# A cross-attention and LoRA kernel on one core: the second batch's codes written in place by ScalarE alone, and half of the turned high part copied by VectorE

## The chip, the cores and the metric

The kernel runs on one core of a Trainium2 chip. The metric is the device time of one execution in microseconds (us), the median of several runs. All times below come from those runs or from one profiled execution.

## What is computed

Two batches of 1024 rows of x (2048 wide) are normalised, quantised to 8 bits and multiplied by a quantised context of 2048 x 2048 for each batch. The product is added to x. The sum is normalised again and goes through four LoRA experts of rank 16, of which a softmax over the two largest router logits weighs two. Cut to what matters:

```python
def fake_quant(x, s, z):
    q = clip(round(x / s + z), 0, 255)
    return (q - z) * s
x = x + tanh(g_xattn) * (fake_quant(layernorm(x)) @ fake_quant(ctx))
flat = layernorm(x)
logits = flat @ Wr.T
gates  = softmax(top 2 of logits, others -inf)
mid    = einsum('tf,erf->ter', flat, A)
delta  = sum_e gates[e] * einsum('ter,eor->teo', mid, B)[e] * 4
x = x + tanh(g_ffn) * delta
```

## The kernel before

**Tiles.** The 2048 rows of x are 16 tiles of 128 rows; tiles 0 to 7 belong to batch 0, tiles 8 to 15 to batch 1. `xr` is a ring of 5 buffers (`RING`): tile b lives in buffer b % 5, is loaded there, gets the product added (`add_main`, L1197), then the LoRA part (`add_delta`, L1269), and is stored from there. So tile b + 5 can be loaded only when tile b is stored: `load_x` (L247) waits for `out_stored`, and the store for `out_ready`, which `add_delta` counts. All DMAs are issued by SyncE from one list (L272 to L355), in its order.

**The product.** For each tile 16 slices of the context (k) by 4 column blocks (n) of 512 are accumulated in PSUM (`product`, L668). The operands are whole numbers in f16: the codes of x less their centre, transposed (`q1T`), and those of the context (`q2`). Tiles 0 to 3 are worked on together, slice by slice, while the context of batch 0 arrives (`rows`, L676); from tile 4 on, tile by tile (`main`, L689).

**The context rows.** A context of one batch is 32 half slices of 128 x 1024 f32, here called rows 0 to 63 (`place`, L163). A row is loaded to a staging unit (`stage`, L241: 16 units within batch 1's own part of `q2`, and one in `q1T`), ScalarE rounds it to bytes in the low halves of the 16-bit words of `c_code`, whose high halves hold 1024's pattern (`scale_row`, L443), and VectorE subtracts 1024 and the centre and writes f16 to `q2` (`code_row`, L1136). A unit is loaded again once its row is scaled. Rows 32 to 63 are needed from tile 8 on.

**x to `q1T`.** VectorE takes the statistics of x (`stats_x` for each half, L1141; `var_x`), GpSimd the power -1/2 (`power_x`, L374), VectorE the scale (`scale_of_x`, L1153); ScalarE writes the bytes (`scale_x`, L449), TensorE transposes them (`turn_q1`, L645), and ScalarE, for tiles 0 and 1 VectorE, copies them out of PSUM (`copy_q1T`, L455).

**The low-rank stage of a tile.** After `add_main`: `stats_h`, `var_h`, GpSimd's `power_h`, `bias_h` on VectorE. ScalarE writes the high part in f16 (`high_part`, L464) and the f32 value in halves (`normal_half`, L473), GpSimd the low part (`low_part`, L383). TensorE transposes both parts by halves (`turn_hi`, `turn_lo`), ScalarE copies both halves of the high part and half 0 of the low one to `hT` (`copy_hiT`, `copy_loT`, L479 to L487), VectorE half 1 of the low one (L1220). TensorE multiplies by A (`mid_hi`, `mid_lo`), VectorE ranks the gates (`rank_gates`, L1228), ScalarE takes the exponential (`gate_exp`, L489), VectorE weighs (`weigh`, L1246), TensorE transposes the gated middle (`turn_gate`, L738), VectorE splits it (`split_gate`), TensorE multiplies by B (`delta`, L748) and VectorE adds (`add_delta`). `delta(b, n)` waits until the adds up to `(b, n - 2)` are done, since it has two PSUM banks.

**The order** on every engine is written out by hand up to tile 8 and is a loop from tile 9 (`STEADY`) on. An engine works through its list strictly in order, so what stands behind a waiting step waits too.

## Time and profile before

| | us |
|---|---|
| median of 3 runs | 375.06 |
| lowest and highest | 374.97, 376.85 |
| the profiled execution | 376.49 |
| its span, first to last instruction | 374.7 |
| TensorE busy (share of the span) | 337.6 (90%) |
| VectorE busy | 290.2 (77%) |
| ScalarE busy | 251.0 (67%) |
| GpSimd busy | 96.8 (26%) |

The engines are called PE (TensorE; PEld its weight loads), DVE (VectorE), ACT (ScalarE), POOL (GpSimd) and SP (SyncE) in the rows. A row of a timeline gives the start, the duration, the engine, the line, the operation, what it writes and reads, how many alike follow one another, and in brackets the idle time before it and what ended that. Successive matmuls overlap, so their durations are longer than the distance from one start to the next. PEclk is the granted TensorE clock as a share of the full one. Idle time of an engine costs something only if the work that sets the end waits for it.

### The profile page before, as it was taken

To read this page: it belongs to the slowest core of one execution; us is meant where nothing else is said; L and a number is where in the kernel's file an instruction comes from. 1 tells how busy PE (TensorE), PEld (TensorE's weight loads), DVE (VectorE), ACT (ScalarE), POOL (GpSimd) and SP (SyncE) were. 2 spreads that over 40 slices of the span, in tenths; PEclk is the share of its full clock that TensorE was granted. 3 is DMA by queue.
4 is the path that set the end of the run, shared out by engine and by line. 5 is a ranking of instruction groups with operands and counts; after the bars stand their busy time and mean duration, and the time that the engine had idled before them with its cause. 6 is when DMAs were issued, how large, how long until landed. Compare 5 with 4: busy or idle time off the path is not lost. (4 is left out here: it accounts for less than half of the span.)

```text
span 374.7 us, 6441 instructions
## 1 busy us (share of the span) xinstructions
PE 337.6 (90%) x2372; PEld 188.7 (50%) x2372; DVE 290.2 (77%) x715; ACT 251.0 (67%) x207; POOL 96.8 (26%) x107
## 2 busy tenths in 40 slices
PE   0579989999985789999989999999999999999984
PEld 0234434445653665455555556464656565555552
DVE  4785889589996799999947796968686877866685
ACT  1769848949999699689898147464747473756150
POOL 3100430005545322033043222140505050505000
PEclk9999999999998599999999999999999999999999
DMA  7999999960046769672570524141405020202023
GB/s 218 415 420 419 420 420 420 417 278 2 3 148 239 268 247 359 213 260 87 172 258 1 193 107 152 56 170 57 170 34 192 2 115 1 114 0 114 0 86 140
DMA packets 19185, 69.17 MB, mean 185 GB/s; under 512 B 2256, under 2 KB 2256, under 8 KB 19024
## 3 DMA queue, kind: packets, MB, share of 16 engines
q1 hardware_dynamic: 19152, 68.73, 48.4%
q8 instruction: 21, 0.34, 0.4%
q14 instruction: 12, 0.10, 0.1%
HBM read 51.94 MB, written 16.78 MB: 183 GB/s over the span
## 5 line engine op out<-in xcount | busy, mean ns | idle before, releaser
L671 PE MATMUL ps_main<-q,q1T 128*128 128x512 f16 x832 | 197.4, 379 | 2.2 <-ACT q1T L460 1.6
L671 PEld LDWEIGHTS ps_main<-q,q1T 128*128 128x128 f16 x832 | 77.4, 98 | 87.2 <-issue 9.0
L446 ACT ACTIVATE c_code<-q,small_tile 128x1024 uint8<-128x1024 f32 x62 | 74.7, 1239 | 25.0 <-DVE q L1139 13.7
L470 ACT ACTIVATE h_parts<-xr,small_tile 128x2048 f16<-128x2048 f32 x15 | 31.4, 2094 | 39.4 <-DVE small_tile L1217 39.4
L390 POOL TENSOR_TENSOR h_parts<-work,h_parts 128x512 f16<-128x512 f32 x30 | 34.8, 1180 | 66.3 <-ACT work L476 66.3
L1139 DVE TENSOR_SCALAR q<-c_code,small_tile 128x1024 f16<-128x1024 f16 x64 | 37.0, 580 | 14.0 <-ACT c_code L446 13.6
L1200 DVE SCALAR_TENSOR_TENSOR xr<-ps_main,small_tile,xr 128x512 f32<-128x512 f32 x52 | 38.6, 743 | 8.1 <-PE ps_main L671 8.0
L1144 DVE BATCH_NORM_STATS2 small_tile<-xr 128x6 f32<-128x512 f32 x64 | 40.9, 680 | 5.2 <-DMA xr<-in_x 5.2
L1205 DVE BATCH_NORM_STATS2 small_tile<-xr 128x6 f32<-128x512 f32 x64 | 43.6, 687 | 0.9
L1273 DVE TENSOR_TENSOR xr<-ps_delta,xr 128x512 f32<-128x512 f32 x62 | 41.2, 680 | 3.9 <-PE ps_delta L756 3.2
L381 POOL TENSOR_TENSOR small_tile<-small_tile 128x1 f32<-128x1 f32 x16 | 9.3, 583 | 128.3 <-DVE small_tile L1213 128.3
L482 ACT COPY hT<-ps_turn 128x1024 f16<-128x1024 f16 x32 | 31.4, 1006 | 12.5 <-PE ps_turn L708 12.4
L452 ACT ACTIVATE x_byte<-xr,small_tile 128x2048 uint8<-128x2048 f32 x16 | 33.5, 2092 | 7.8 <-DVE small_tile L1159 7.8
L390 POOL TENSOR_TENSOR h_parts<-q1T,h_parts 128x512 f16<-128x512 f32 x30 | 34.1, 1160 | 1.3 <-ACT q1T L476 1.3
L754 PE MATMUL ps_delta<-lora_bT,gT_hi 128*128 128x512 f32 x60 | 30.1, 502 | 0.4 <-DVE gT_hi L1265 0.3
L460 ACT ACTIVATE q1T<-ps_gate,small_tile 128x2048 f16<-128x2048 uint8 x12 | 23.6, 1964 | 8.0 <-PE ps_gate L654 8.0
L756 PE MATMUL ps_delta<-lora_bT,gT_lo 128*128 128x512 f32 x60 | 24.4, 406 | 0.0
L642 PE MATMUL ps_main<-ident_h 128*128 128x512 f16 x47 | 12.9, 421 | 12.2 <-issue 12.2
L376 POOL TENSOR_TENSOR small_tile<-small_tile 128x1 f32<-128x1 f32 x16 | 9.5, 595 | 53.7 <-DVE small_tile L1151 53.7
L1223 DVE COPY hT<-ps_turn 128x1024 f16<-128x1024 f16 x16 | 11.0, 687 | 15.4 <-PE ps_turn L715 15.4
L671 PE MATMUL ps_turn<-q,q1T 128*128 128x512 f16 x64 | 18.1, 380 | 4.8 <-DVE q L1139 3.1
L727 PE MATMUL ps_mid<-a_parts,hT 128*128 128x136 f16 x256 | 20.8, 229 | 0.9 <-ACT hT L482 0.9
(122 smaller groups left out, 415.1 us busy)
## 6 DMA issues: line engine op xcount, KB each, us to landing
q<-in_ctx SPq DMA_DIRECT2D x62, 512.0 KB, 10.9
xr<-in_x SPq DMA_DIRECT2D x32, 512.0 KB, 4.9
out_x<-xr SPq DMA_DIRECT2D x30, 512.0 KB, 3.4
h_parts<-in_B SPq DMA_DIRECT2D x1, 1024.0 KB, 16.5
q1T<-in_ctx SPq DMA_DIRECT2D x2, 512.0 KB, 6.4
out_x<-xr SPq DMA_DIRECT2D x4, 256.0 KB, 2.3
xr<-in_A SPq DMA_DIRECT2D x1, 544.0 KB, 16.2
small_tile<-in_params SPq DMA_DIRECT2D x1, 3.0 KB, 2.6
```

Source lines behind the costliest of these rows:

```text
L390: nc.gpsimd.tensor_tensor(h_lo[:, half(h)][:, part], work[h][:, part], h_hi[:, half(h)][:, part], ALU.subtract).then_inc(h_lo_ready, 1)
L446: nc.scalar.activation(c_byte[:, i % 2, :], stage(i), ACT.Identity, bias=par[:, 3:4], scale=inv_s[:, 1:2]).then_inc(row_scaled, 1)
L452: nc.scalar.activation(x_byte[:, :], xr[:, b % RING, :], ACT.Identity, bias=q_scale[:, 1:2], scale=q_scale[:, 0:1]).then_inc(x_scaled, 1)
L470: nc.scalar.activation(h_hi[:, :], xr[:, b % RING, :], ACT.Identity, bias=h_bias[:, b % 2:b % 2 + 1], scale=h_rstd[:, b % 2:b % 2 + 1]).th ...
L482: nc.scalar.copy(hT[:, h, :, :], as16(ps_turn[h], F16).rearrange("p (k m) -> p k m", m=P)).then_inc(hiT_ready, 1)
L671: mm = pe.matmul(product_bank(b, n)[:, :], q1T_of(b)[:, k, :], q2[:, batch(b), k, cols(n)], start=(k == 0), stop=(k == KT - 1))
L754: pe.matmul(ps_delta[n % 2][:, :], gT_hi[:, :], lora_bT[:, cols(n)], start=True, stop=False)
L1139: nc.vector.tensor_scalar(q2[:, batch_of, k, half(h)], c_code[:, i % 2, :], low_centre[:, :], None, ALU.add).then_inc(row_coded, 1)
L1144: nc.vector.bn_stats(x_stats[:, n, :], xr[:, b % RING, cols(n)]).then_inc(x_stats_done, 1)
L1200: nc.vector.scalar_tensor_tensor(out=x1, in0=product_bank(b, n)[:, :], scalar=gain[:, 0:1], in1=x1, op0=ALU.mult, op1=ALU.add).then_inc(x1 ...
L1205: nc.vector.bn_stats(h_stats[:, b % 2, n, :], xr[:, b % RING, cols(n)]).then_inc(h_stats_done, 1)
L1273: nc.vector.tensor_tensor(x1, src[:, :], x1, ALU.add).then_inc(out_ready, 1)
```

## The change

Three things change, and with them the lists of all engines.

1. **Codes of batch 1.** Rows 32 to 63 are no longer coded by VectorE. GpSimd fills each of batch 1's 16 slices of `q2` with a pattern that is 1024 in both f16 halves (`clear`), and ScalarE writes the bytes straight into the low halves, so `q2` holds 1024 + code. The product of batch 1 is then too large by (1024 + centre) times the sum of the tile's x codes less their centre, one number for each row of x. ScalarE sums the codes (`sum_codes`, two activations a tile with an accumulator), VectorE makes the shift (`shift_of_row`), and `add_delta` subtracts it for tiles 8 to 15. Since the number is constant along a row, it drops out of the second normalisation.
2. **Staging.** Eight units in `q2`, one in `c_code` and one in `q1T` serve rows 32 to 63 (18 units in all with batch 0's). The slices of batch 1 lie in the order `slot_of`; slices 8 to 15 are cleared first, the others when their units are empty (`left_by`).
3. **The turned high part.** Half 1 of it is copied by VectorE (`copy_hiT` on VectorE), half 0 by ScalarE as before.

```diff
-            def copy_hiT(b, h):
-                act.wait_ge(hi_turned, 2 * b + h + 1)
-                wait(act, lo_used, 2 * (b - 1) + h + 1)
-                nc.scalar.copy(hT[:, h, :, :], as16(ps_turn[h], F16).rearrange("p (k m) -> p k m", m=P)).then_inc(hiT_ready, 1)
+            def copy_hiT(b):
+                act.wait_ge(hi_turned, 2 * b + 1)
+                wait(act, lo_used, 2 * b - 1)
+                nc.scalar.copy(hT[:, 0, :, :], as16(ps_turn[0], F16).rearrange("p (k m) -> p k m", m=P)).then_inc(hiT_ready[0], 1)
...
+            def copy_hiT(b):
+                dve.wait_ge(hi_turned, 2 * b + 2)
+                wait(dve, lo_used, 2 * b)
+                nc.vector.tensor_copy(hT[:, 1, :, :], as16(ps_turn[1], F16).rearrange("p (k m) -> p k m", m=P)).then_inc(hiT_ready[1], 1)
...
+            def clear(k):
+                pool.wait_ge(row_scaled, left_by[k])
+                nc.gpsimd.memset(q2_pair[:, slot_of[k], :], TWO_BASES).then_inc(place_cleared, 1)
...
             def scale_row(i):
                 act.wait_ge(row_loaded[unit_of[i]], 16 * (unit_turn(i)[1] + 1))
-                wait(act, row_coded, i - 1)
-                nc.scalar.activation(c_byte[:, i % 2, :], stage(i), ACT.Identity,
+                batch_of, k, h = place(i)
+                if batch_of == 0:
+                    wait(act, row_coded, i - 1)
+                    byte = c_byte[:, i % 2, :]
+                else:
+                    act.wait_ge(place_cleared, k + 1)
+                    byte = q2_byte[:, slot_of[k], half(h), 0]
+                nc.scalar.activation(byte, stage(i), ACT.Identity,
                                      bias=par[:, 3:4], scale=inv_s[:, 1:2]).then_inc(row_scaled, 1)
...
+            def sum_codes(b):
+                act.wait_ge(x_scaled, b + 1)
+                wait(act, row_summed, b - PER_B)
+                for h in range(2):
+                    wait(act, codes_summed, 2 * (b - PER_B) + h)
+                    nc.scalar.activation(byte_copy[:, :], x_byte[:, half(h)], ACT.Identity, bias=0.0, scale=1.0,
+                                         accum_out=code_sums[:, h:h + 1]).then_inc(codes_summed, 1)
...
+            def shift_of_row(b):
+                dve.wait_ge(codes_summed, 2 * (b - PER_B) + 2)
+                nc.vector.scalar_tensor_tensor(out=row_sum[:, :], in0=code_sums[:, 0:1], scalar=code_sums[:, 1:2], in1=x_zeros[:, :],
+                                               op0=ALU.add, op1=ALU.add).then_inc(row_summed, 1)
+                dve.wait_ge(row_summed, b - PER_B + 1)
+                nc.vector.tensor_scalar(shift[:, b % RING:b % RING + 1], row_sum[:, :], code_gain[:, :], None, ALU.mult).then_inc(shift_ready, 1)
...
-                nc.vector.tensor_tensor(x1, src[:, :], x1, ALU.add).then_inc(out_ready, 1)
+                if b < PER_B:
+                    nc.vector.tensor_tensor(x1, src[:, :], x1, ALU.add).then_inc(out_ready, 1)
+                else:
+                    dve.wait_ge(shift_ready, b - PER_B + 1)
+                    nc.vector.scalar_tensor_tensor(out=x1, in0=src[:, :], scalar=shift[:, b % RING:b % RING + 1], in1=x1,
+                                                   op0=ALU.subtract, op1=ALU.add).then_inc(out_ready, 1)
```

The unit numbers of rows 32 to 63, by which loads wait:

```diff
-        late_unit = (8, 9, 10, 11, 12, 13, 14, 15, 16, 13, 14, 15, 14, 15, 15, 16)
-        unit_of = [i % KT for i in range(3 * KT)] + list(late_unit)
+        late_unit = (0, 1, 2, 3, 4, 5, 6, 7, 16, 17, 0, 1, 2, 3, 4, 5, 16, 17, 0, 1, 2, 3, 16, 17, 0, 1, 16, 17, 16, 17, 16, 17)
+        unit_of = [i % KT for i in range(2 * KT)] + list(late_unit)
```

The list of SyncE around the first stores was `load_row(47)`, `store(0, 0)`, `load_row(48)`, `store(0, 1)`, `load_x(5)`, `load_row(49)`, and is now `load_row(52)`, `store(0, 0)`, `store(0, 1)`, `load_row(53)`, `load_x(5)`.

How the lists moved is shown at three places. The first is VectorE where it first meets x of tile 5 (`BN_STATS ... x2` is one `stats_x`, the rows on `ps_delta` are `add_delta`, `hT` is a copy out of PSUM). Before:

```order
L1139 TENSOR_SCALAR q2<-c_code,small_tile 128x1024
L1273 TENSOR_TENSOR xr<-ps_delta0,xr 128x512
L1273 TENSOR_TENSOR xr<-ps_delta1,xr 128x512
L1217 TENSOR_SCALAR small_tile<-small_tile 128x1
L1144 BN_STATS small_tile<-xr 128x6 x2
L1273 TENSOR_TENSOR xr<-ps_delta0,xr 128x512
L1223 COPY hT<-ps_turn1 128x1024
L1273 TENSOR_TENSOR xr<-ps_delta1,xr 128x512
L1144 BN_STATS small_tile<-xr 128x6 x2
```

and after the change:

```order
L1323 CAST gT_hi<-ps_gate 128x128
L1325 TENSOR_TENSOR gT_lo<-ps_gate,gT_hi 128x128
L1197 BN_STATS small_tile<-xr 128x6 x2
L1332 TENSOR_TENSOR xr<-ps_delta0,xr 128x512
L1276 COPY hT<-ps_turn1 128x1024
L1332 TENSOR_TENSOR xr<-ps_delta1,xr 128x512
L1270 TENSOR_SCALAR small_tile<-small_tile 128x1
L1332 TENSOR_TENSOR xr<-ps_delta0,xr 128x512
```

The code of a row is gone, and the statistics of x5 moved from behind the two adds of tile 1 to ahead of them and of the copy.

The second is TensorE ahead of the first product of tile 5 (`ps_main0<-q2,q1T`; `x_byte` is `turn_q1(5)`, `gated` is `turn_gate(3, 6)`). Before:

```order
L754 MATMUL ps_delta1<-lora_bT,gT_hi 128x512
L756 MATMUL ps_delta1<-lora_bT,gT_lo 128x512
L654 MATMUL ps_gate<-ident_h,x_byte 128x128 x8
L708 MATMUL ps_turn0<-ident_h,h_parts 128x128 x8
L708 MATMUL ps_turn1<-ident_h,h_parts 128x128 x8
L671 MATMUL ps_main0<-q2,q1T 128x512 x5
L746 MATMUL ps_gate<-ident_f,gated 128x128
L671 MATMUL ps_main0<-q2,q1T 128x512
L727 MATMUL ps_mid<-a_parts,hT 128x136 x8
```

and after the change:

```order
L753 MATMUL ps_turn0<-ident_h,h_parts 128x128 x8
L780 MATMUL ps_mid<-a_parts,hT 128x68 x8
L753 MATMUL ps_turn1<-ident_h,h_parts 128x128 x8
L699 MATMUL ps_gate<-ident_h,x_byte 128x128 x8
L772 MATMUL ps_mid<-a_parts,hT 128x136 x8
L791 MATMUL ps_gate<-ident_f,gated 128x128
L772 MATMUL ps_mid<-a_parts,hT 128x136 x8
L760 MATMUL ps_turn0<-ident_h,h_parts 128x128 x8
L716 MATMUL ps_main0<-q2,q1T 128x512 x4
L799 MATMUL ps_delta0<-lora_bT,gT_hi 128x512
```

The middle products of tile 4, the gate of tile 3 and a transpose of tile 4's low part moved ahead of tile 5's first product.

The third is ScalarE from the low part of tile 3 (`hT<-ps_turn0`) to `copy_q1T(5)` (`q1T<-ps_gate`); `x_byte` is `scale_x(5)`, `mids` is `gate_exp(3)`, `h_parts` is `high_part(4)`. Before:

```order
L487 COPY hT<-ps_turn0 128x1024
L452 ACTIVATE x_byte<-xr,small_tile 128x2048
L470 ACTIVATE h_parts<-xr,small_tile 128x2048
L491 ACTIVATE small_tile<-mids,small_tile 128x4
L460 ACTIVATE q1T<-ps_gate,small_tile 128x2048
```

and after the change:

```order
L541 COPY hT<-ps_turn0 128x1024
L524 ACTIVATE h_parts<-xr,small_tile 128x2048
L497 ACTIVATE x_byte<-xr,small_tile 128x2048
L536 COPY hT<-ps_turn0 128x1024
L530 ACTIVATE work0<-xr,small_tile 128x1024
L545 ACTIVATE small_tile<-mids,small_tile 128x4
L514 ACTIVATE q1T<-ps_gate,small_tile 128x2048
```

The high part of tile 4 moved ahead of `scale_x(5)`, and a copy and a half of tile 4 moved ahead of `copy_q1T(5)`; `gate_exp(3)` stands ahead of it in both.

## Rows read from the trace of the kernel before

**Rows 1.** Page, part 1: busy time and share of the span, each engine

```profile
PE 337.6 (90%) x2372; PEld 188.7 (50%) x2372; DVE 290.2 (77%) x715; ACT 251.0 (67%) x207; POOL 96.8 (26%) x107
```

**Rows 2.** Timeline of PE: start us, duration us, what, [idle before]

```profile
108.53 2.10 PE L671 MATMUL ps_main<-q,q1T 128*128 128x512 f16 x9
...
121.78 0.64 PE L735 MATMUL ps_mid<-a_parts,hT 128*128 128x68 f16 x8 [3.81 <-DVE hT L1223]
...
126.61 0.48 PE L746 MATMUL ps_gate<-ident_f,gated 128*128 128x128 f32 x1 [2.49 <-DVE gated L1257]
...
136.29 1.24 PE L671 MATMUL ps_main<-q,q1T 128*128 128x512 f16 x5 [1.26 <-ACT q1T L460]
```

**Rows 3.** Windows: stretch, length, busy per engine, PEclk, DMA share, GB/s

```profile
115.00:125.00 10.00, 4.79 (x52) 3.61 (x48) 6.71 (x19) 7.31 (x8) 4.68 (x5) 0.70 0.93 342
```

**Rows 4.** Timeline of DVE around the statistics of x5

```profile
107.72 0.67 DVE L1273 TENSOR_TENSOR xr<-ps_delta,xr 128x512 f32<-128x512 f32 x1
...
119.25 1.28 DVE L1144 BATCH_NORM_STATS2 small_tile<-xr 128x6 f32<-128x512 f32 x2 [3.16 <-DMA xr<-in_x]
...
121.64 0.68 DVE L1273 TENSOR_TENSOR xr<-ps_delta,xr 128x512 f32<-128x512 f32 x1
...
123.43 0.29 DVE L1230 TENSOR_REDUCE ps_mid<-ps_mid 128x68 f32<-128x136 f32 x1
...
124.79 0.26 DVE L1149 BATCH_NORM_AGGREGATE small_tile<-small_tile 128x2 f32<-128x24 f32 x1
```

**Rows 5.** Timeline of ACT, steady part

```profile
338.28 2.10 ACT L470 ACTIVATE h_parts<-xr,small_tile 128x2048 f16<-128x2048 f32 x1 [5.24 <-DVE small_tile L1217]
```

**Rows 6.** Groups by line and form: busy us, mean ns, idle before

```profile
L446 ACT ACTIVATE c_code<-q,small_tile 128x1024 uint8<-128x1024 f32 x62 | 74.7, 1239 | 25.0 <-DVE q L1139 13.7 <-DMA q<-in_ctx 11.3
...
L1273 DVE TENSOR_TENSOR xr<-ps_delta,xr 128x512 f32<-128x512 f32 x62 | 41.2, 680 | 3.9 <-PE ps_delta L756 3.2 <-PE ps_delta L767 0.6
...
L1200 DVE SCALAR_TENSOR_TENSOR xr<-ps_main,small_tile,xr 128x512 f32<-128x512 f32 x52 | 38.6, 743 | 8.1 <-PE ps_main L671 8.0
L1139 DVE TENSOR_SCALAR q<-c_code,small_tile 128x1024 f16<-128x1024 f16 x64 | 37.0, 580 | 14.0 <-ACT c_code L446 13.6
...
L482 ACT COPY hT<-ps_turn 128x1024 f16<-128x1024 f16 x32 | 31.4, 1006 | 12.5 <-PE ps_turn L708 12.4
...
L1223 DVE COPY hT<-ps_turn 128x1024 f16<-128x1024 f16 x16 | 11.0, 687 | 15.4 <-PE ps_turn L715 15.4
...
L360 POOL MEMSET c_code<- 128x2048 f16 x1 | 1.8, 1804 | 0.3 <-POOLq L1597 0.3
```

**Rows 7.** DMA, us to landing, issued at 108.42, 132.47, 106.51, 114.05, 126.83

```profile
out_x<-xr SPq DMA_DIRECT2D x1, 512.0 KB, 5.6
...
out_x<-xr SPq DMA_DIRECT2D x1, 512.0 KB, 3.7
...
out_x<-xr SPq DMA_DIRECT2D x1, 512.0 KB, 2.6
...
xr<-in_x SPq DMA_DIRECT2D x1, 512.0 KB, 5.2
...
xr<-in_x SPq DMA_DIRECT2D x2, 512.0 KB, 4.6
```

**Rows 8.** Timeline of PE, steady part: middle product of two tiles

```profile
327.11 0.64 PE L727 MATMUL ps_mid<-a_parts,hT 128*128 128x136 f16 x8
...
346.86 0.64 PE L727 MATMUL ps_mid<-a_parts,hT 128*128 128x136 f16 x8
347.34 0.61 PE L715 MATMUL ps_turn<-ident_h,h_parts 128*128 128x128 f16 x8
```

**Rows 9.** Timeline of DVE: a slow `code_row`

```profile
47.56 2.48 DVE L1139 TENSOR_SCALAR q<-c_code,small_tile 128x1024 f16<-128x1024 f16 x1
```

**Rows 10.** Waits of PE: waited for, us in total, times, longest

```profile
PE ps_main L671 <- ACT q1T L460: 1.6, 2, 1.3
...
PE ps_mid L727 <- ACT hT L482: 0.9, 1, 0.9
```

715 lines of the change are left out of this document (359 added, 356 removed).

## Prediction

> **What bounds the kernel now.** The page first: TensorE is busy for 90% of the span and VectorE for 77% [rows 1], so a change that takes work off VectorE pays only where TensorE waits for it. The timeline of TensorE shows where that is. From tile 9 on it runs almost without a gap, 19.8 us a tile (the first middle product of one tile starts at 327.11, that of the next at 346.86 [rows 8]), and nothing that this change does there can move the end. The one large hole lies between the last product of tile 4, issued until 110.5 us [rows 2], and the first of tile 5 at 136.29 [rows 2]; in it TensorE works only on the low-rank stage of tiles 1 to 4, with waits of 3.81, 2.49 and 1.26 us. The window over its worst part adds that the granted clock was 0.70 there in the mean [rows 3]; 1.00 is the level of 2.4 GHz and 0.50 that of 1.2 GHz, and the fall came after the engine had stood idle behind its wait of 3.81 us. The hole costs some 10 us of idleness and some 4 of half speed.
>
> What ends the hole is tile 5's x. It goes into the ring buffer of tile 0, so it is a round trip: the last `add_delta` of tile 0 (107.72 us, ends 108.39), the store, the load, the statistics at 119.25 after a wait of 3.16 us for the DMA [rows 4], then the scale, ScalarE's `scale_x(5)`, the transposes and ScalarE's `copy_q1T(5)`. Tiles 6 and 7 take the same trip. I count from T, the time at which VectorE finds the first half of x5: T = 119.25 before, and tile 5 starts at T + 17.0.
>
> **What hides and what does not.** Removed: 32 `code_row` of 0.58 us = 18.6 us of VectorE, and 16 ScalarE copies of 1.01 = 16.1 us. Added: 16 VectorE copies of 0.69 = 11.0 us [rows 6], and 16 `sum_codes` activations of 1024 elements, for which the nearest row is the coding activation of as many elements, 1.24 us [rows 6]: 20 us of ScalarE, most of it in the steady part, where that engine stands idle 5.24 us before each tile's high part [rows 5]. I cost both at nothing; the cover is TensorE's 19.8 us a tile, and if it were gone each pair would cost 2.5 us. The 16 clears on GpSimd have one near row, a memset of 2048 elements in 1.80 us [rows 6]; a clear has half the elements and as many bytes, so 0.9 to 1.8 us, and I take 0.95. Ten fall before the hole ends, in time GpSimd has idle, ahead of low parts which then wait for ScalarE anyway: nothing.
>
> Up to 85 us the new order gains little. The early x scales come before waiting rows, which brings tile 1 forward by 1.5 us, but tiles 2 and 3 start 2 us later, and VectorE's work on B is as long as before. I make the start of tile 4 0.6 us earlier (between 1.5 earlier and 1.5 later). It is lost again at once, because of the next term.
>
> **The step that decides.** ScalarE now scales rows 42 to 44 before `copy_loT(1)`; eight more products stand ahead of tile 0's last delta. Counting TensorE from 86.0 us (0.6 before the 86.6 of now) with 0.22 us a product (nine in 2.10 [rows 2]), I get the last `add_delta` of tile 0 at 108.5, as before. The store then takes between 3.7 us and 5.6 (a context row was issued just ahead of that one; now row 53 comes just behind the store), the load 4.6 to 5.2 [rows 7]. So T lies at 116.9 to 119.5; I take 117.5, nearer the short end since nothing is ahead of the store.
>
> But VectorE's order around T is another one. Before, `stats_x(5, 0)` stood behind `add_delta(1, 0)` and `(1, 1)`; now it stands ahead of both and of `copy_loT(2)`. They are ready 3 us before T and are queued behind a DMA. After T come: statistics 1.2, add 0.6, copy 0.6, add 0.6, bias 0.15, add 0.6, `rank_gates(2)` 1.36 (from 123.43 to 124.79 [rows 4]), add 0.65: `add_delta(1, 3)` ends at T + 5.8. Before it ended at 122.32, which is T + 3.1 [rows 4]. So x6, whose load waits for tile 1's store, comes at T + 5.8 + 3.7 + 4.6 and some issue time = T + 14.7. `stats_x(6, 0)` again stands ahead of the last `add_delta` of its round, of `rank_gates(3)`, `copy_hiT(4)` and `weigh(3)`. ScalarE has `gate_exp(3)` ahead of `copy_q1T(5)`, and TensorE has `turn_gate(3, 6)`, `mid_hi(4, 1)` and `turn_lo(4, 0)` ahead of tile 5. That makes: x6 T + 14.7, statistics 1.2, but VectorE, with TensorE at half speed, arrives a little later: add ends T + 17.4, rank 18.8, copy 19.4, weigh 20.3, then gate transpose 0.17, middle product 0.48 (346.86 to 347.34 [rows 8]) and transposes 0.45, in all 1.1. Tile 5 starts at T + 21.4 = 138.9, 2.6 us later than before. Work that stood behind this point is now ahead of it: two middle products 0.96, a gate 0.17, one set of transposes 0.45 = 1.6 us. **Term 1: 2.6 - 1.6 = +1.0 us.**
>
> The third trip: `add_delta(2, 3)` ends at T + 17.4, x7 lands at T + 25.9, `stats_x(7, 0)` stands ahead of `add_delta(3, 0)`, which ends at T + 27.8. TensorE reaches `delta(3, 2)`, which waits for it, at T + 25.0 and holds the rest of tile 5's first block behind it. Before, the third load was issued early enough. **Term 2: +2.8 us.**
>
> After this TensorE finds everything ready: x8 and x9 have room, and low parts and copies of hi come earlier, so TensorE's wait of 0.9 us for ScalarE's copy of hi goes, and the shorter of the two for q1T (1.6 in sum, the longer 1.3: 0.3) [rows 10]. **Term 3: -1.2 us.** In the tail the copy on VectorE replaces the second ScalarE copy, which was hidden by an add; and the last adds take the form with a scalar, 0.74 in place of 0.68 us [rows 6] (three of tile 14 and the four last). **Term 4: +0.4 us.**
>
> Sum +3.0. The profiled execution took 376.49 us (span 374.7), 1.4 above the median of 375.06, so it would become 379.5 and the median **378.0 us**.
>
> **A rule weighed.** One `code_row` took 2.48 us at 47.56 [rows 9], the mean is 0.58 [rows 6], and in the slow one GpSimd was working. So the clears between 66 and 76 us could lengthen the last `code_row`s of batch 0. TensorE needs row 31 at 77.4 us and it is coded at 74.6, so 2.8 us are covered; five clears of 0.95 that each hold a code back cost 4.8 - 2.8 = 2.0 us. The Trainium skill ("SBUF — State Buffer", section "SBUF: two separate sides") calls the pair of ports that VectorE and GpSimd share an exclusive lock: whichever starts first keeps the pair for its whole instruction and the other blocks. By this rule the clears would block VectorE, and the sum would be +5.0, not +3.0, if all five collided; by the rows each one meets a short instruction now and then, so I leave it at nothing.
>
> **Rivals.**
> - *The round trips are short (faster).* A store took 2.6 us when nothing ran beside it [rows 7]. With stores of 2.6 and loads of 3.8 each trip is 1.9 us shorter than I took. T = 115.6, tile 5 at T + 19.3 = 134.9, so term 1 is -3.0, term 2 +0.9, with terms 3 and 4 a sum of -2.9: 372.2 us. If VectorE never waited for x at all (trip under 5.1 us, the work between `add_delta(0, 3)` and `stats_x(5, 0)`), tile 5 starts at 131 and it is 367 us. For it: VectorE does lose 18.6 us of work in the stretch where it was fullest. Against: x5 took 10.9 us from add to statistics. It turns at trips of 7.3 us. Chance 0.22.
> - *No change that can be measured.* Trips about 1 us shorter than taken, or the start gains its 1.5 us, 375 us. Chance 0.20.
> - *My forecast,* 0.40, own range 376.9 to 380.
> - *The clock stays low.* Before, it fell after a wait of 3.81 us [rows 2, 3] and was full again when tile 5 began. In the new order TensorE idles 4 us (T + 16 to 20) just before tile 5, so its first products may run at 1.2 GHz and take twice the time. Work of 3 us at half speed adds 3: 381 us. Chance 0.12.
> - *The port lock,* 380 us. Chance 0.06.
>
> **How the numbers follow.** A measurement of this kernel can tell 0.5%, 1.9 us, from no change. Slower: 0.40 + 0.12 + 0.06 = 0.58. Same 0.20, faster 0.22. The range reaches down to the short trips and up to the low clock with 1 us more for the landing of x5; it leaves out a VectorE that never waits, and above 382 a low clock together with a collision at the port.
>
> **What would show it.** VectorE's `stats_x(5, 0)`, `(6, 0)` and `(7, 0)` waiting for DMA by 3 to 4, up to 2, and 2 to 3 us; the first product of tile 5 near 139 us and `delta(3, 2)` waiting for VectorE's add; GpSimd's memset near 0.95 us; nothing of 32 late `code_row`; tiles 9 to 15 at 19.8 us each. I am wrong if tile 5 starts before 135 us, or if x7 has landed when VectorE comes to it. If tiles 9 to 15 take longer than 19.8 us each, `sum_codes` or the shift is not hidden.

## The result and the profile after

The change makes the kernel slower: median 380.79 us of 4 runs (379.26 to 382.64) against 375.62 of 4 of the kernel before (374.97 to 376.85); ratio 1.0142, 95% interval 1.0118 to 1.0166, so +5.2 us where 2.9 were forecast (378.0 against 375.06). The profiled execution after took 379.26 us (span 377.4), the one before 376.49: +2.8 between the two profiles, forecast +3.0. The median of 380.79 lies above the own range of the forecast, 376.9 to 380. Executions more than 1.5% above the fastest of their kernel are left out of all ratios; there are three, in three kernels below, and each is named with its time. Two things need an explanation: where the time between the two profiles goes, and why the medians differ by more than the profiles do.

The page's busy times, to hold against [rows 1]:

```profile
PE 337.2 (89%) x2372; PEld 188.4 (50%) x2372; DVE 291.5 (77%) x717; ACT 254.3 (67%) x223; POOL 110.1 (29%) x123
```

VectorE is as busy as before (290.2 then) although 32 codes left it. They took only 14.5 us with them (37.0 before, 22.5 now), and the 16 copies added 10.9, the two small operations of `shift_of_row` 3.4 and the longer adds 2.0. Its timeline where it waits for a load of x or ends tile 0, to hold against [rows 4]:

```profile
106.62 1.50 DVE L1332 TENSOR_TENSOR xr<-ps_delta,xr 128x512 f32<-128x512 f32 x2 [0.16 <-PE ps_delta L801]
...
116.72 1.29 DVE L1197 BATCH_NORM_STATS2 small_tile<-xr 128x6 f32<-128x512 f32 x2 [3.31 <-DMA xr<-in_x]
...
131.91 1.29 DVE L1197 BATCH_NORM_STATS2 small_tile<-xr 128x6 f32<-128x512 f32 x2 [2.68 <-DMA xr<-in_x]
...
141.79 1.29 DVE L1197 BATCH_NORM_STATS2 small_tile<-xr 128x6 f32<-128x512 f32 x2 [2.04 <-DMA xr<-in_x]
...
155.84 1.29 DVE L1197 BATCH_NORM_STATS2 small_tile<-xr 128x6 f32<-128x512 f32 x2 [2.03 <-DMA xr<-in_x]
...
170.59 1.29 DVE L1197 BATCH_NORM_STATS2 small_tile<-xr 128x6 f32<-128x512 f32 x2 [3.95 <-DMA xr<-in_x]
```

Before, one such wait stood here (3.16 us); now there are five, for x5 to x9. TensorE's timeline, to hold against [rows 2, 8, 10]:

```profile
111.73 0.62 PE L760 MATMUL ps_turn<-ident_h,h_parts 128*128 128x128 f16 x8 [2.74 <-POOL h_parts L402]
...
118.75 0.47 PE L799 MATMUL ps_delta<-lora_bT,gT_hi 128*128 128x512 f32 x1 [1.76 <-DVE xr L1332]
...
124.63 0.33 PE L791 MATMUL ps_gate<-ident_f,gated 128*128 128x128 f32 x1 [2.62 <-DVE gated L1315]
...
136.81 1.07 PE L772 MATMUL ps_mid<-a_parts,hT 128*128 128x136 f16 x8 [5.62 <-DVE gated L1315]
...
139.64 1.28 PE L716 MATMUL ps_main<-q,q1T 128*128 128x512 f16 x4
...
143.81 0.47 PE L799 MATMUL ps_delta<-lora_bT,gT_hi 128*128 128x512 f32 x1 [0.16 <-DVE xr L1332]
...
158.52 0.47 PE L799 MATMUL ps_delta<-lora_bT,gT_hi 128*128 128x512 f32 x1 [1.32 <-DVE xr L1332]
...
329.73 0.64 PE L772 MATMUL ps_mid<-a_parts,hT 128*128 128x136 f16 x8
...
349.48 0.64 PE L772 MATMUL ps_mid<-a_parts,hT 128*128 128x136 f16 x8
```

TensorE waits 1.76 us for an add that was queued behind x5, 2.62 and 5.62 for gates queued behind x5 and x6, 1.32 for an add behind x8. Tile 5's first product is at 139.64 (before 136.29). In the steady part one tile still takes 349.48 - 329.73 = 19.75 us. Windows, the first as in [rows 3]:

```profile
115.00:125.00 10.00, 5.38 (x60) 3.77 (x60) 8.04 (x23) 8.68 (x8) 5.68 (x6) 0.94 0.65 229
...
132.00:140.00 8.00, 3.19 (x26) 2.96 (x27) 7.14 (x25) 5.09 (x6) 3.73 (x4) 0.58 0.67 233
```

The clock is higher than before from 115 to 125 (0.94 against 0.70) and is low later, 0.58 from 132 to 140, just ahead of tile 5. The groups that answer to [rows 6]:

```profile
L1332 DVE TENSOR_TENSOR xr<-ps_delta,xr 128x512 f32<-128x512 f32 x32 | 21.5, 680 | 3.1 <-PE ps_delta L801 2.9
...
L1335 DVE SCALAR_TENSOR_TENSOR xr<-ps_delta,small_tile,xr 128x512 f32<-128x512 f32 x30 | 21.6, 742 | 0.6 <-PE ps_delta L812 0.6
...
L1184 DVE TENSOR_SCALAR q<-c_code,small_tile 128x1024 f16<-128x1024 f16 x32 | 22.5, 707 | 7.4 <-ACT c_code L490 7.2
...
L506 ACT ACTIVATE byte_copy<-x_byte 128x1024 uint8<-128x1024 uint8 x16 | 16.8, 1050 | 0.3
...
L1281 DVE COPY hT<-ps_turn 128x1024 f16<-128x1024 f16 x16 | 10.9, 682 | 0.8 <-PE ps_turn L753 0.7
...
L408 POOL MEMSET q<- 128x1024 f32 x16 | 15.3, 969 | 26.3 <-ACT c_code L490 16.3 <-ACT q L490 10.0
```

A ledger of TensorE made from each trace says where the time went. It has the idle times in the brackets of its timeline, summed by stretch, and for the half clock the sum over 1 us windows of busy time x (1 - PEclk). The first stretch ends with the wait ahead of tile 4's first product (at 86.61 before, near 85.5 in the others). Stretches with a difference, us:

| profile (span) | idle 0-87 | idle 87-111 | idle 111-144 | half clock 111-144 | idle 144-165 | idle 165-200 |
|---|---|---|---|---|---|---|
| before (374.7) | 18.7 | 0.2 | 9.3 | 4.2 | 0.0 | 1.2 |
| changed (377.4) | 17.4 | 0.0 | 13.7 | 3.4 | 1.3 | 0.4 |
| changed, repeated (378.5) | 17.7 | 0.0 | 12.9 | 4.8 | 1.3 | 1.7 |
| four places undone (372.3, its fastest execution) | 17.0 | 0.0 | 9.2 | 4.4 | 0.8 | 0.2 |

Over the whole span the two kinds of loss add up to 36.5, 38.8, 40.9 and 34.1 us: differences to before of +2.3, +4.4 and -2.4, where the spans differ by +2.7, +3.8 and -2.4. The ledger accounts for the spans within 0.6 us. The changed kernel gains 1.3 us up to the start of tile 4, and loses more than that in the hole and just behind it.

### The profile page after: what moved, and what is told of

Same layout as the page of the kernel before. It is cut to its first block, busy times and chain, and to the rows that moved or that the text cites. A ratio compares the mean times of both kernels' runs of the same rounds, so it can differ in the third digit from the quotient of the medians.

```text
span 377.4 us, 6514 instructions
## 1 busy us (share of the span) xinstructions
PE 337.2 (89%) x2372; PEld 188.4 (50%) x2372; DVE 291.5 (77%) x717; ACT 254.3 (67%) x223; POOL 110.1 (29%) x123
## 4 chain that ended last, share of the span: by engine, by line
PE 61%; DMA 16%; DVE 14%; SPq 5%; issue 2%; ACT 1%; DVEq 0%; ACTq 0%
PE ps_main L716 38%; DMA xr<-in_x 6%; DMA out_x<-xr 5%; DMA xr<-in_A 4%; SPq L280 4%; PE ps_mid L772 3%; PE ps_turn L760 3%; PE ps_turn L753 3%; PE ps_delta L799 3%; PE ps_delta L801 3%; DVE small_tile L1197 3%; PE ps_turn L716 2%; DVE xr L1332 2%; DVE xr L1253 2%; PE ps_delta L716 2%
## 5 line engine op out<-in xcount | busy, mean ns | idle before, releaser
L402 POOL TENSOR_TENSOR h_parts<-work,h_parts 128x512 f16<-128x512 f32 x30 | 34.1, 1160 | 65.2 <-ACT work L530 65.2
L1197 DVE BATCH_NORM_STATS2 small_tile<-xr 128x6 f32<-128x512 f32 x64 | 40.9, 680 | 15.3 <-DMA xr<-in_x 15.3
L490 ACT ACTIVATE c_code<-q,small_tile 128x1024 uint8<-128x1024 f32 x32 | 38.4, 1237 | 17.1 <-DMA q<-in_ctx 9.0
L393 POOL TENSOR_TENSOR small_tile<-small_tile 128x1 f32<-128x1 f32 x16 | 8.8, 550 | 108.9 <-DVE small_tile L1266 108.9
L402 POOL TENSOR_TENSOR h_parts<-q1T,h_parts 128x512 f16<-128x512 f32 x30 | 34.1, 1160 | 1.5 <-ACT q1T L530 1.5
L1184 DVE TENSOR_SCALAR q<-c_code,small_tile 128x1024 f16<-128x1024 f16 x32 | 22.5, 707 | 7.4 <-ACT c_code L490 7.2
L536 ACT COPY hT<-ps_turn 128x1024 f16<-128x1024 f16 x16 | 16.1, 1003 | 14.0 <-PE ps_turn L753 14.0
L687 PE MATMUL ps_main<-ident_h 128*128 128x512 f16 x47 | 12.9, 424 | 12.5 <-issue 12.5
L1332 DVE TENSOR_TENSOR xr<-ps_delta,xr 128x512 f32<-128x512 f32 x32 | 21.5, 680 | 3.1 <-PE ps_delta L801 2.9
L490 ACT ACTIVATE q<-q,small_tile 128x1024 uint8<-128x1024 f32 x20 | 23.7, 1232 | 0.0
L772 PEld LDWEIGHTS ps_mid<-a_parts,hT 128*128 128x128 f16 x256 | 18.0, 103 | 10.1 <-issue 5.8
L408 POOL MEMSET q<- 128x1024 f32 x16 | 15.3, 969 | 26.3 <-ACT c_code L490 16.3
```

The source lines that it names most:

```text
L402: nc.gpsimd.tensor_tensor(h_lo[:, half(h)][:, part], work[h][:, part], h_hi[:, half(h)][:, part], ALU.subtract).then_inc(h_lo_ready, 1)
L490: nc.scalar.activation(byte, stage(i), ACT.Identity, bias=par[:, 3:4], scale=inv_s[:, 1:2]).then_inc(row_scaled, 1)
L772: mm = pe.matmul(ps_mid[:, 0:2 * J], hT[:, h, k, :], a_parts[:, kk, :, :].rearrange("p c j -> p (c j)"), start=(kk == 0), stop=False)
L1197: nc.vector.bn_stats(x_stats[:, n, :], xr[:, b % RING, cols(n)]).then_inc(x_stats_done, 1)
L1332: nc.vector.tensor_tensor(x1, src[:, :], x1, ALU.add).then_inc(out_ready, 1)
```

## The experiments

All times are medians; the kernel before was run beside each group (375.15 to 375.63 us in the medians of five groups).

**The changed kernel again.** No edit.

> The changed kernel, unchanged, once more. Its profiled execution took 379.26 us and the three others 380.45 to 382.64, at mean granted clocks of 0.984 and 0.976 to 0.982, while the profiled execution of the kernel before was at 0.982. Two explanations of why the medians differ by 5.2 us where the two profiles differ by 2.8. (a) Clock: in the long hole before tile 5 TensorE's clock stays at its lower level for longer in some executions; then a longer execution shows a lower mean clock, 1 us longer for each 0.003 of it (0.003 x 377), and its extra time lies between 110 and 150 us. (b) The transfers of x land later in some executions; then the clock says nothing and the waits of VectorE for x5 to x8 (3.31, 2.68, 2.04, 2.03 us) are longer in the new profile. I expect (a) in part: median 380.5 (379.3 to 382), lower clocks with the longer executions.

Measured: 379.98 us (379.62 to 380.22), ratio 1.0121 (1.0103 to 1.0140). The clock does not order its executions: 380.22 us at 0.986, 380.11 at 0.977. So (a), the clock, falls. The profile equals the first one within 0.5 us up to 169 us and is then 1.1 us later through one place. VectorE and TensorE:

```profile
171.68 1.29 DVE L1197 BATCH_NORM_STATS2 small_tile<-xr 128x6 f32<-128x512 f32 x2 [4.99 <-DMA xr<-in_x]
```

```profile
143.90 0.47 PE L799 MATMUL ps_delta<-lora_bT,gT_hi 128*128 128x512 f32 x1 [0.58 <-DVE xr L1332]
...
158.58 0.47 PE L799 MATMUL ps_delta<-lora_bT,gT_hi 128*128 128x512 f32 x1 [1.29 <-DVE xr L1332]
...
176.43 0.65 PE L772 MATMUL ps_mid<-a_parts,hT 128*128 128x136 f16 x8 [1.46 <-DVE hT L1281]
```

x9 was found at 171.68 (170.59 in the first profile, above), the copy of tile 5's high part is queued behind it, and TensorE waited 1.46 us for the copy, in the first profile not at all. A fifth wait on x costs nothing or a microsecond, depending on the load. That speaks for (b).

**One place of VectorE's list undone.**

```diff
-            stats_x(5, 0)
             add_delta(1, 0)
             copy_loT(2)
             add_delta(1, 1)
+            stats_x(5, 0)
```

> Only the first of the four places is undone: VectorE's statistics of the first half of x5 stand behind both adds and the copy that are ready, as in the kernel before. Theory (head of line): the adds (1,0) to (1,2) and the copy no longer wait 3.31 us; add (1,3) ends about 2 us sooner, at about T + 3.5 in place of T + 5.7, the load of x6 is issued at 124.3 in place of 126.3, and x6 lands 2 us sooner, so that VectorE's wait at x6 shrinks from 2.68 to about 1 and tile 5 starts at 137.5 in place of 139.64: 2 us less than the repeated kernel. Rival (the landing of x5 alone counts, since TensorE's hole is ended by x5's own path): the start of tile 5 moves by less than 0.5 us, and the time by less than 0.5 us.

Measured: 379.42 (377.99 to 382.58), ratio 1.0124 (1.0091 to 1.0157): the median is 0.6 less than that of the repeated kernel, but by the ratios (1.0121 there) the two are not told apart. x5 is no longer waited for and x6 hardly, as the theory said:

```profile
130.23 1.29 DVE L1197 BATCH_NORM_STATS2 small_tile<-xr 128x6 f32<-128x512 f32 x2 [0.29 <-DMA xr<-in_x]
...
140.42 1.29 DVE L1197 BATCH_NORM_STATS2 small_tile<-xr 128x6 f32<-128x512 f32 x2 [2.34 <-DMA xr<-in_x]
...
143.47 1.29 DVE L1197 BATCH_NORM_STATS2 small_tile<-xr 128x6 f32<-128x512 f32 x2 [1.18 <-DMA xr<-in_x]
...
155.47 1.29 DVE L1197 BATCH_NORM_STATS2 small_tile<-xr 128x6 f32<-128x512 f32 x2 [1.98 <-DMA xr<-in_x]
```

But x7 and its second half are now waited for 2.34 and 1.18 us, where the repeated kernel waited 2.13: the first middle product of tile 4 came 1.7 us sooner (135.12 against 136.79) and most of that was lost again at the next x. The theory's mechanism holds, its gain of 2 us does not.

**Four places undone.**

```diff
-            stats_x(6, 0)
             add_delta(2, 3)
             rank_gates(3)
             copy_hiT(4)
             weigh(3)
+            stats_x(6, 0)
...
-            stats_x(7, 0)
             add_delta(3, 0)
-            stats_x(7, 1)
             add_delta(3, 1)
+            stats_x(7, 0)
+            stats_x(7, 1)
...
-            stats_x(8, 0)
             add_main(5, 2)
             add_delta(4, 0)
             stats_h(5, 2)
             add_delta(4, 1)
+            stats_x(8, 0)
```

and x5's as above.

> All four places: the statistics of the first halves of x5, x6, x7 and x8 stand behind the work that is ready (two adds and a copy; an add, the ranking, a copy and the weighing; two adds; an addition of the product, two adds and their statistics). No wait goes, only what is queued behind it. Theory: the three trips are each shorter by what their last add waited for, tile 5 starts at about 137, TensorE's waits of 1.32 at delta (4, 2) and 0.16 at delta (3, 2) go; 4 us less than the repeated kernel, so about 376.5, 1 us above the kernel before. Rival 1 (the order of VectorE is not what costs: DMA landings or ScalarE's and TensorE's own orders hold tile 5 back): within 1 us of the repeated kernel. Rival 2 (x is now found later, its scale comes later, and ScalarE waits): slower than the repeated kernel by 1 to 2 us.

Measured: 375.82 (374.10 to 378.26, and one of 380.59), ratio 1.0018 (0.9995 to 1.0040): 4.2 us less than the repeated kernel, where 4 were expected. Both rivals fall. Of VectorE's waits for x5 to x8 0.33 us is left, and TensorE's hole is shorter:

```profile
116.71 1.29 DVE L1197 BATCH_NORM_STATS2 small_tile<-xr 128x6 f32<-128x512 f32 x2 [0.33 <-DMA xr<-in_x]
```

```profile
121.28 1.03 PE L760 MATMUL ps_turn<-ident_h,h_parts 128*128 128x128 f16 x8 [3.02 <-POOL h_parts L402]
...
132.87 0.63 PE L772 MATMUL ps_mid<-a_parts,hT 128*128 128x136 f16 x8 [2.49 <-DVE gated L1315]
...
135.27 1.91 PE L716 MATMUL ps_main<-q,q1T 128*128 128x512 f16 x4
```

Every instruction, place in memory and load is as in the changed kernel; only what stood behind the statistics of a late x now stands ahead. So the order of VectorE's list was the whole loss, as far as the runs can tell (the interval of this ratio takes in 1).

**Part 3 undone.** A `copy_hiT1` on ScalarE takes half 1 of the high part, behind `normal_half(b, 1)` (tile 4: `(4, 0)`), and VectorE's copies go.

> Only part 3 of the change is undone: half 1 of the turned high part is copied by ScalarE again (16 x 1.0 us), everything else and every other place in the lists as in the changed kernel. Theory: both engines have room in the steady part, so tiles 9 to 15 stay at 19.8 us; in the hole VectorE saves two copies of 0.69 that stand ahead of the weighing of tiles 2 and 3 while ScalarE gets two of 1.0 beside a wait of 2.0 us: within 1 us of the repeated kernel. Rival (the copy belongs to what costs the time, since VectorE is full in the hole): 1 to 1.5 us less than the repeated kernel. Rival (it is this part that pays, ScalarE being the later one): 1 to 3 us more.

Measured: 384.88 (382.45 to 385.43), ratio 1.0252 (1.0230 to 1.0273): 4.9 more, 2.2 between the two profiles. The theory falls and the last rival holds: in the order of the changed kernel, and with ScalarE's copy placed as here, this part pays. Its size is above what that rival said (1 to 3), and over half of it lies outside the profile. TensorE waits twice for ScalarE's copy of half 1 (L541 is the new `copy_hiT1`), of tiles 5 and 6:

```profile
176.39 0.65 PE L787 MATMUL ps_mid<-a_parts,hT 128*128 128x136 f16 x8 [0.52 <-ACT hT L541]
...
192.96 0.65 PE L787 MATMUL ps_mid<-a_parts,hT 128*128 128x136 f16 x8 [2.12 <-ACT hT L541]
```

The first of them stands where the repeated kernel waited 1.46 us for VectorE's copy, so only the second is new. Besides, the first middle product of tile 4 began 1.0 us later (137.77 against 136.79).

**Five places undone**: behind x5 to x8 also x9.

```diff
-            stats_x(9, 0)
             add_main(6, 1)
-            stats_x(9, 1)
             stats_h(6, 1)
-            var_x(9)
             copy_hiT(5)
+            stats_x(9, 0)
+            stats_x(9, 1)
+            var_x(9)
```

> As the kernel with four places undone, and a fifth: both halves of the statistics of x9 stand behind the second addition of tile 6's product, its statistics and the copy of tile 5's high part. In the profile of the repeated kernel VectorE waited 4.99 us for x9 (3.95 in the changed kernel's first profile), ended at 171.68 (170.59), and TensorE waited 1.46 us for the copy behind it (not at all in the first profile): the 1.1 us between these two executions. Theory: this fifth wait is why executions of the same kernel differ, so with it harmless the median comes down to the lowest execution of the four-place kernel, 374.3 (median there 375.8, lowest 374.1), and the executions lie closer together: under 1.5 us between the lowest and the next to highest. Rival (the spread is the clock's or the transfers' elsewhere): median 375.8 again, spread as wide.

Measured: 375.90 (374.60 to 379.64), ratio 1.0024 (0.9996 to 1.0051). The rival holds: the median is unchanged and the spread no narrower, although the profile shows no wait of VectorE for x at all. Once the other four were in order, x9 did not matter.

**TensorE kept busy in the hole.**

```diff
+                pe.wait_ge(x1_ready, parts_done(4, 2))
+                keep_busy(9)
                 turn_lo(2, 0)
...
+                keep_busy(9)
                 turn_lo(3, 0)
...
+                keep_busy(8)
                 mid_hi(4, 0)
```

> As the kernel with five places undone, and TensorE is kept busy in its hole with 9, 9 and 8 products of 512 columns into a bank that is free (ahead of the transposes of the low parts of tiles 2 and 3, where it waits 2.74 and 3.02 us for GpSimd, and ahead of tile 4's first middle product, where it waits 2.49 us): 0.22 us each, 2.0 us a time at 2.4 GHz. In the four-place kernel the granted clock was at half from 121 to 127 and from 134 to 137 us, some 9 us of which TensorE worked some 7. If the half clock costs what it seems (work that takes twice as long, 3.5 us, part of it hidden in waits): 1.5 to 3 us less than the five-place kernel, and a mean clock of 0.99. Rival (the chain through ScalarE and GpSimd sets the hole, and TensorE's work in it is beside the path): within 0.5 us. Rival (a product that is issued late holds the transposes back): up to 1 us more.

Measured: 376.13 (375.65 to 378.48), ratio 1.0023 (1.0003 to 1.0044), no gain. Windows of this kernel, then of the one with five places:

```profile
126.00:140.00 14.00, 12.31 (x120) 8.13 (x119) 11.02 (x32) 13.57 (x11) 5.07 (x5) 0.98 0.68 237
```

```profile
126.00:140.00 14.00, 11.45 (x94) 8.35 (x94) 11.05 (x31) 13.26 (x11) 5.07 (x5) 0.78 0.71 254
```

The granted clock rose from 0.78 to 0.98 in the second half of the hole, the mean of the execution from 0.979 to 0.993, and the time did not follow. Tile 4's first middle product did begin 1.1 us earlier (132.99 against 134.09), but in this profile x7 came late again: VectorE waited 1.64 and 0.78 us for it and TensorE 1.65 us for a copy behind it, which the other profile does not have. That TensorE's work in the hole stands beside the path fits the medians; whether the products held x7 back or it was late by itself was not tested.

**The first clears twice.**

```diff
+                if k < 8:
+                    nc.gpsimd.memset(q2_pair[:, slot_of[k], :], TWO_BASES).then_inc(first_clear, 1)
+                    pool.wait_ge(first_clear, k + 1)
                 nc.gpsimd.memset(q2_pair[:, slot_of[k], :], TWO_BASES).then_inc(place_cleared, 1)
```

> The changed kernel with the first eight clears done twice, eight more memsets of 0.95 us on GpSimd between 62 and 76 us, where VectorE codes the last rows of batch 0. Theory (as forecast: the clears cost nothing): within 0.5 us of the repeated kernel, start of tile 4 at 85.5 to 86.0. Rival (GpSimd and VectorE shut each other out): code_row, which rose from 580 to 707 ns in the mean with eight clears beside it, rises again by some 100 ns, tile 4 starts 0.5 to 2 us later and the kernel takes as much more.

Measured: 381.12 (380.48 to 383.37), ratio 1.0148 (1.0122 to 1.0175), about 1 us more than the repeated kernel, tile 4 at 86.49 in place of 85.55. That is the rival's size, but not its cause: the codes took 656 ns in the mean, less than 707. The profile shows the microsecond in GpSimd's queue:

```profile
69.45 0.21 DVE L1213 TENSOR_SCALAR small_tile<-small_tile 128x1 f32<-128x1 f32 x1 [2.44 <-POOL small_tile L389]
...
73.39 0.55 DVE L1188 TENSOR_SCALAR q<-c_code,small_tile 128x1024 f16<-128x1024 f16 x1 [1.63 <-ACT c_code L494]
```

`power_x(4)` stands behind the clears, VectorE waited 2.44 us for it (0.43 in the repeated kernel) and ScalarE's `scale_x(4)` 1.78 us (there not at all). What clear and code do to each other stands in single rows. In the repeated kernel ScalarE's semaphore released both at once, and the code (VectorE) took 1.25 us where 0.47 is usual, the clear (GpSimd) 0.95:

```profile
73.73 1.25 DVE L1184 TENSOR_SCALAR q<-c_code,small_tile 128x1024 f16<-128x1024 f16 x1 [0.21 <-ACT c_code L490]
```

```profile
73.76 0.95 POOL L408 MEMSET q<- 128x1024 f32 x1 [0.51 <-ACT c_code L490]
```

With clears back to back the code at 73.39 began first and took 0.55; the clear that began beside it took the longer time:

```profile
73.60 1.23 POOL L410 MEMSET q<- 128x1024 f32 x1
```

**Without the sums.** The subtraction of each row's constant is left out for batch 1 (`sum_codes`, `shift_of_row`, and `add_delta` in its plain form).

> The changed kernel without ScalarE's sums of codes, without the shift and with the plain add everywhere: the subtraction of the constant of each row is left out for batch 1. Theory (both hidden in the steady part, 0.4 us in the tail): 0 to 0.6 us less than the repeated kernel, tiles 9 to 15 at 19.8 us each in both. Rival (the wait of VectorE for the sum of tile 8 or ScalarE's 2.3 us ahead of copy_loT(5) and copy_hiT(6) cost something between 165 and 195 us): 1 to 2 us less, and TensorE's waits of up to 0.3 us there gone.

Measured: 380.74 (378.91 to 382.15), ratio 1.0127 (1.0101 to 1.0153): no difference that can be told, against 1.0121. The sums are hidden, as the theory said.

**Loads of x first.** On the kernel with five places:

```diff
-            load_row(56)
             store(2, 0)
             store(2, 1)
             load_x(7, 0)
             load_x(7, 1)
+            load_row(56)
```

> As the kernel with five places undone, and on SyncE the load of row 56 stands behind the stores of tile 2 and the load of x7 in place of ahead of them (issued near 137 in place of 125.4 us; ScalarE scales it at 149.4). In the profile of the kernel with five places x7 had landed when VectorE came to it, in that with keep-busy products it had not: a wait of 1.64 us at 139.97 and of 0.78 for its second half, with the copy of tile 4's low part behind them and TensorE behind that for 1.65 us. Theory (the executions of these kernels differ by when x7 lands, and its round trip shares the queue with x6's load and row 56): the store of tile 2 lands 1 us sooner, x7 too, and the executions come together near the lowest of the five-place kernel: median 375.0 (it was 375.9, lowest 374.6), spread under 1.5 us without one outlier. Rival (the spread is elsewhere): median 375.9, executions from 374.6 to 379 as before.

Measured: 375.77 (373.41 to 376.57), ratio 0.9998 (0.9978 to 1.0018). Four executions were below 374.3, three of them lower than any until then, eight above 375.6: unclear, nearer the rival.

**ScalarE's rows behind the halves.** On the kernel with five places:

```diff
-            scale_row(45)
             normal_half(2, 0)
             copy_hiT(2)
+            scale_row(45)
...
-            scale_row(48)
             normal_half(3, 0)
             copy_hiT(3)
+            scale_row(48)
```

> As the kernel with five places undone, and ScalarE scales rows 45 and 48 behind the first half of the normalised value and the copy of the high part of tiles 2 and 3, in place of ahead of them. TensorE's two longest waits of the hole now are for GpSimd's low parts of these tiles (2.76 us at 111.68, 2.60 at 121.61), GpSimd waits for ScalarE's half, and ScalarE is busy without a gap. Theory (ScalarE's list sets the hole once VectorE's doesn't): each of the two waits is shorter by the 1.13 us of a row, everything to tile 5 comes 1 to 2 us sooner: median 374.3 (373.5 to 375). Rival (x5 and x6, not the low parts, set when tile 5 starts): within 0.5 us of 375.9.

Measured: 377.43 (375.94 to 380.53, and one of 382.22), ratio 1.0060 (1.0033 to 1.0088): 1.5 more. TensorE's waits for the low parts did shrink (1.61 and 1.87 us), but x5, its load issued at 112.29, was found 1.7 us later than with four places undone (118.44 against 116.71), and the weighing is still behind it. The edit has a side effect that I had not seen: row 53 is loaded to the staging unit of row 45, so its load waits until row 45 is scaled. It went out at 110.31 in place of 108.44, right ahead of x5's. The kernel with both edits shows the same (row 53 at 110.41, x5 found at 119.17).

```profile
118.44 1.29 DVE L1197 BATCH_NORM_STATS2 small_tile<-xr 128x6 f32<-128x512 f32 x2 [2.19 <-DMA xr<-in_x]
```

```profile
124.55 0.47 PE L791 MATMUL ps_gate<-ident_f,gated 128*128 128x128 f32 x1 [3.63 <-DVE gated L1315]
```

**Part 3 alone**, on the kernel before: `copy_hiT` of half 1 on VectorE, placed near the times of ScalarE's copies.

> The kernel before with part 3 of the change alone: half 1 of the turned high part is copied by VectorE (16 copies of 0.69 us in place of 16 of 1.0 on ScalarE), its codes and their places as before. Taking this part out of the changed kernel cost 4.9 us (384.9 against 380.0). Theory (ScalarE is the busiest engine from 86 to 126 us, 25.00 of 25 and 12.06 of 15 us, so its copies stand on the path): 1 to 4 us less than the kernel before. Rival (VectorE is as full there, 23.4 of 25 us, and its copy delays the adds by which x5 comes in): within 1 us of it. Rival (the 4.9 us belonged to the order of the changed kernel alone): 1 to 2 us more than before.

Measured: 378.24 (376.98 to 379.58), ratio 1.0083 (1.0063 to 1.0103): 2.9 more than before. TensorE waited for my first placement, behind a code and statistics, and tile 5 then began as late as before the change:

```profile
95.34 0.65 PE L717 MATMUL ps_mid<-a_parts,hT 128*128 128x136 f16 x8 [2.84 <-DVE hT L1218]
...
136.54 1.24 PE L661 MATMUL ps_main<-q,q1T 128*128 128x512 f16 x5 [1.26 <-ACT q1T L460]
```

So this part's worth hangs on its place in the list; alone and placed like this it costs, in the changed kernel it pays. The profiled execution took 376.98 us, only 0.5 more than the one before, so where most of the 2.9 lies is not shown.

**The last two edits together** (loads first, rows behind).

> The last two edits together on the kernel with five places undone: row 56 loaded behind x7, rows 45 and 48 scaled behind the halves. If both theories hold, 373.5 and the lowest of all kernels here, faster than the kernel before by 0.5%. If only ScalarE's order counts, as the kernel with that edit alone; if neither, 375.9.

Measured: 376.54 (375.64 to 378.68), ratio 1.0037 (1.0021 to 1.0053): neither theory.

**x6, x7 and x8 undone, x5 left.**

> The changed kernel with the places of x6, x7 and x8 undone and that of x5 left. With x5's place alone undone the time was 379.4 (0.6 less than the repeated kernel), with all four 375.8. Theory (each late x holds back the adds by which the next x comes, and x6's place holds the most: an add, the ranking, a copy and the weighing): most of the 4.2 us come back, median 377 (376.3 to 377.8), tile 5's first middle product near 135.5 in place of 136.8. Rival (only all four together help, since any one left moves the wait on): above 378.5. Rival (x5's place costs nothing beside the others): 375.8.

Measured: 378.36 (377.36 to 379.83), ratio 1.0083 (1.0059 to 1.0108). x5's place alone gives 0.6 (within the noise), the other three 1.6, all four 4.2. They do not add. The profile fits the reading that one late x that is left in the way holds the next ones back: VectorE waits 2.74 us for x5 and again 2.60 for x7, and TensorE then 1.78 for the copy behind x7.

**Row 53 behind x5's load**, on top of row 56's place.

> As the kernel with five places undone and row 56 behind x7's load (median 375.8; executions in two groups, four from 373.4 to 374.3 and eight from 375.6 to 376.6), and also row 53 behind the load of x5 (it is scaled near 141 us). x5's first half landed 4.6 to 6.6 us after its load was issued at 112.1 to 112.8. Theory (row 53's transfer, issued at 108.5 beside the store, and x5 share the 16 DMA engines; the two groups are an early and a late x5): x5 lands near 4.6 us after its issue in all executions, which move to the lower group: median 374.0. Rival (the groups come from elsewhere, or the store alone sets it): 375.8 in two groups.

Measured: 375.25 (373.87 to 379.22), ratio 1.0002 (0.9979 to 1.0026). The groups have run into each other; 0.5 less is within what can be told. Its profile, of an execution of 376.49, shows a loss elsewhere. ScalarE:

```profile
156.72 1.24 ACT L490 ACTIVATE q<-q1T,small_tile 128x1024 uint8<-128x1024 f32 x1 [4.29 <-DMA q1T<-in_ctx]
...
162.70 1.24 ACT L490 ACTIVATE q<-q1T,small_tile 128x1024 uint8<-128x1024 f32 x1 [1.66 <-DMA q1T<-in_ctx]
...
163.85 2.08 ACT L497 ACTIVATE x_byte<-xr,small_tile 128x2048 uint8<-128x2048 f32 x1
```

TensorE:

```profile
165.98 0.62 PE L699 MATMUL ps_gate<-ident_h,x_byte 128*128 128x128 f16 x8 [2.28 <-ACT x_byte L497]
```

ScalarE waited for two rows' loads, x8's scale stood behind the second, and TensorE waited 2.28 us for it.

**x5 behind the weighing**, on top: `stats_x(5, 0)` and `(5, 1)` behind `weigh(2)` and `copy_hiT(3)`.

> As the kernel just before, and both halves of x5's statistics stand behind the weighing of tile 2 and the copy of tile 3's high part, so that no ranking or weighing is queued behind x5. Theory: the time no longer depends on when x5 lands up to about 120 us; TensorE's wait for the gate of tile 2 (1.25, 1.75, 3.63, 4.26 us in four profiles, in the order of x5's landing) is under 1 us, x5's scale is as early as before since ScalarE is at the high part of tile 4 till 127: median 374.0, spread under 1.5 us. Rival (x5's own path is now 1 to 2 us later and tile 5 waits for it): 376 to 377.

Measured: 375.72 (373.40 to 376.45), ratio 1.0003 (0.9986 to 1.0020). The wait for the gate of tile 2 went, and TensorE waited 2.43 us for the split of that gate instead. Theory and rival are both half right; no gain.

**And ScalarE's rows behind the halves**, on top.

> As the kernel just before, and rows 45 and 48 scaled behind the halves and copies of tiles 2 and 3, the edit that made 377.4 of 375.9 before. Theory (it failed there because x5, which then stood ahead of the weighing, landed late, and TensorE waited 3.63 us for the weighing): now it brings the 1.1 us of a row at TensorE's two waits for GpSimd: median 373.0, faster than the kernel before by over 0.5%. Rival (the edit costs by itself, for example by holding back the rows' loads): 1 us or more above the kernel just before.

Measured: 376.46 (374.56 to 377.90), ratio 1.0028 (1.0009 to 1.0046). The rival: that edit costs by itself, here with row 53 loaded behind x5 and no ranking or weighing queued behind x5.

**x8's scale ahead of row 61's**, on the kernel with rows 53 and 56 moved.

```diff
-            scale_row(61)
             scale_x(8)
+            scale_row(61)
```

> As the kernel with five places undone and rows 56 and 53 behind the loads of x (375.25, profile at 376.49), and ScalarE scales x8 ahead of row 61. There the scale of x8 began at 163.85 after ScalarE had waited 1.66 us for row 61; its factors were ready at 158.9 and ScalarE was free at 161.0. TensorE's turn of x8 waited 2.28 us at 165.98. Theory (in this region a row's load, not x, is what is waited for): the scale begins at 161.0, TensorE's wait goes, high part of tile 5 is as before: 1 to 2 us less, median 373.8, faster than the kernel before by 0.4%. Rival (TensorE's next wait, for the low part of tile 5 behind the high part and row 62, takes it over): within 0.5 us of 375.25.

Measured: 374.93 (373.49 to 376.12, and one of 712.88, which no profile explains), ratio 0.9991 (0.9978 to 1.0004). TensorE's wait at x8 is gone; 0.3 less than without the edit.

**And row 59 loaded ahead of x8.**

> As the kernel just before, and on SyncE row 59 is loaded ahead of x8 in place of behind it: ScalarE waited 4.29 us for row 59 (2.75 to 4.29 in four profiles) and VectorE came to x8 without a wait. Theory: ScalarE's wait for row 59 falls to about 2 us, rows 60 and 61 follow 1 to 2 us sooner, and since the sums, row 62 and tile 5's high part stand behind them the median is 0.5 us below the kernel just before. Rival (x8 lands 1.5 us later and VectorE waits for it at 153.7): 0.5 us above it.

Measured: 374.83 (372.76 to 375.67), ratio 0.9985 (0.9968 to 1.0001), the lowest of all, and not told from the kernel before (its interval reaches 1). ScalarE's wait for row 59 fell to 0.63 us, and a wait of 3.00 for row 60 took its place.

## Why the prediction was wrong, and what in it was right

**Right: sign, place and mechanism.** By the steps of the forecast: tile 4 began at 85.53 (said 86.0); the last add of tile 0 ended at 108.1 (106.62 + 1.50; said 108.5); x5 was found at T = 116.72 after a wait of 3.31 (said 117.5, 3 to 4); x6 at T + 15.2 after 2.68 (said up to 2, landing at T + 14.7); x7 at T + 25.1 after 2.04 (said T + 25.9, 2 to 3). Tile 5 began at 139.64 (said 138.9), a tile of the steady part takes 19.75 us (said 19.8), a clear 969 ns (said 950), and the sums cost nothing. That VectorE's order is the cause is shown, not only read from the profile: four places undone give back 4.2 us of 4.5.

**The first step that failed** is the sentence "After this TensorE finds everything ready: x8 and x9 have room". I followed the round trip for three tiles and stopped. x8 came late (a wait of 2.03, and 1.32 of TensorE behind it), x9 too (3.95, and in the repeated execution 4.99 and 1.46 of TensorE). That is 1.3 us in one profile and 2.8 in the other, where the forecast has nothing.

**The second was the way from the profile to the median.** I took the new median 1.4 us below the new profile, as it was before. But the offset belongs to the execution. The profile before lay above its median, the profile after was the lowest of its four runs. Why executions of these kernels differ is shown in one pair (x9's landing, 1.1 us), and making x9 harmless did not narrow the spread, so the rest is open. The clock does not order them. The size of this error is not firm either: the same kernel run again had a median of 379.98.

**Between the profiles the sum came out (+2.8 for +3.0), and that was luck.** Its terms were off by more, and cancel.

- Term 1 (+1.0) was too small. Tile 5 began 3.35 us later (139.64 for 136.29), which less the 1.6 of work moved ahead is +1.7. Behind the weighing I had a gate, one middle product and transposes, 1.1 us. It is 2.83 us (136.81 to 139.64): the other middle product of tile 4 waits for the weighing as well, and all four ran at half clock.
- That is the mechanism of the rival that I gave 0.12, but it is not what made the kernel slower: from 111 to 144 us the half clock cost 3.4 us in the one profile and 4.8 in the other, and 4.2 before the change.
- Term 2 (+2.8) was hardly there. Tile 5 began later against T, so TensorE waited only 0.16 us for tile 3's add behind x7 (0.58 in the repeated kernel).
- Terms 1 and 2 were 3.8 together and came to 1.9. The ledger agrees: up to 144 us TensorE lost 2.0 us more than before (2.9 in the repeated kernel).
- Term 3 (-1.2): the two waits that it names are gone (0.94 and 0.30 us in the kernel before, at 191.10 and 175.03). In their place stand new ones of 0.43 in one profile and 1.71 in the other, x9's among them.
- Term 4 (+0.4) was about 0.1: from the weighing of tile 14 (VectorE at 356.09, before at 353.47) to the end of the span 21.3 us against 21.2.
- With the 1.3 us behind x8 these come to 2.5, and the spans differ by 2.7.

**The port.** I gave a rival of 380 us a chance of 0.06. Its mechanism is there: a code that is released together with a clear takes 1.25 us in place of 0.47, and one that began first takes 0.55 while the clear takes 1.23 in place of 0.95. By the rule weighed in the forecast (the Trainium skill, "SBUF — State Buffer", section "SBUF: two separate sides") whichever starts first holds the pair of ports for its whole instruction. The second pair of rows agrees; in the first the code's record starts 0.03 us before the clear's (73.73 and 73.76), and yet the code is the longer one, so these rows do not tell which began. Where the clears run, from 62 to 77 us, nine codes took 0.83 us each, and eleven in the same stretch of the kernel before 0.48: some 3.2 us more for VectorE. They cost the kernel nothing as far as seen, since tile 4 began 1.1 us sooner than before. A kernel without clears was not run, so the cover of 2.8 us that I claimed is not measured.

**A reading that was off.** The store of 2.6 us, "when nothing ran beside it", was issued at 106.51, and a row's load went out at 107.90, within it. The price of the short trips rested on it; the forecast's own sum did not.

**Part 3 I costed at nothing.** In the order of the changed kernel it is worth 4.9 us by the medians, 2.2 by the profiles, against ScalarE's copy in the one place tried.

**Left open.** With the order undone the kernel is as fast as before, not faster, whatever else was tried. The losses of the profiles then lie in the low-rank chain of tiles 2 to 4 (TensorE's waits of about 2.8, 2 and 2.5 us for GpSimd and the weighings) and in row loads through two staging units. Which of them would have to go first was not settled. ScalarE's rows behind the halves cost 1.5 us where row 53's late load may have held x5 back, and still 0.7 where it could not; the cause of the latter is open.

## What to carry to other kernels

An engine's list is also a queue behind every transfer in it. A step that waits for a DMA belongs behind all work that is ready, above all behind work that the same transfer's successor needs. Where a late load delays the store that frees the next buffer, follow the round trip until it has caught up, not for the tiles where it was noticed, and undo all such places together: one alone moves the wait on. And a forecast for a median should not inherit the offset of one profiled execution.

## What the runs showed of the hardware

- GpSimd's memset of 128 x 1024 f32 took 0.95 us where it was released together with a VectorE operation of 0.47 us, which then took 1.25; where that operation had begun first, it took 0.55 and the memset 1.23.
- With TensorE kept busy the granted clock rose from 0.78 to 0.98 over 14 us, and the kernel was no faster (376.13 us against 375.90).
- The first half of x5 was found, each time after a wait for it, between 3.7 us (four places undone: issued 112.99, found 116.71) and 6.2 us after the issue of its load (rows behind: 112.29, 118.44), where the load of a context row had gone out 4.6 us ahead of it in the one and 2.0 us in the other.
